# Cross-attention kernel: attention weights of even heads as bytes unpacked on GpSimd, unread TensorE transposes, output biases on TensorE

## The reference, cut to what matters

```python
q = (x @ Wq + bq);  k, v = cond @ Wkv + bkv        # 16 heads of 16 values, 1024 keys
q = _fq_sym(q, axis=-1); k = _fq_sym(k, axis=-1); v = _fq_sym(v, axis=2)
attn = softmax(q @ k.T)                            # per head, 1024 x 1024
attn = _fq_unsigned(attn, axis=-1)                 # attention weights rounded to 0..255, times a scale
out  = (attn @ v) @ Wp + bp
...
return x + (layernorm(x) @ ternary_quantize(Wt).T + bt)
```

## Time and profile before

| | us |
|---|---|
| median of 3 runs (335.58 to 337.09) | 336.85 |
| the profiled execution | 337.5 |
| its span, first to last instruction | 335.7 |
| outside the span | 1.8 |
| first to last exponential of the attention | 129.07 to 301.10, the last ending at 302.30 |
| from there to the end of the span | 33.4 |

### The profile page before, as it was taken

One profiled execution on the slowest core, in us unless ns is written; L12 is line 12 of the kernel. 1 busy time (PEld: TensorE's weight loads), 2 busy tenths in 40 slices (PEclk: granted clock), 3 DMA queues, 4 the chain that ended last, 5 costly groups with the idle time before them and its releaser, 6 DMA issues.

```text
span 335.7 us, 5142 instructions
## 1 busy us (share of the span) xinstructions
PE 268.7 (80%) x1728; PEld 127.3 (38%) x1728; DVE 265.7 (79%) x401; ACT 210.0 (63%) x340; POOL 98.3 (29%) x225
## 2 busy tenths in 40 slices
PE   4993597595156947899999999999999999979670
PEld 4441365473034733233333332333333333338560
DVE  3363799968697878999999899899999999973850
ACT  1100125435533178999999999999999999992210
POOL 2350424476603011221222212222222122211634
PEclk9999559987555977555555555555555555558998
DMA  7824000039100001999999999999999999995011
GB/s 255 276 94 126 0 3 0 0 59 161 34 0 0 0 2 37 196 182 206 185 200 178 215 172 212 184 212 164 227 167 219 197 188 190 199 184 109 16 49 63
DMA packets 148618, 43.34 MB, mean 129 GB/s; under 512 B 143216, under 2 KB 147696, under 8 KB 148592
## 3 DMA queue, kind: packets, MB, share of 16 engines
q1 hardware_dynamic: 146496, 39.60, 65.4%
q0 software_dynamic: 768, 2.10, 1.8%
q10 hardware_dynamic: 1328, 1.32, 1.2%
HBM read 5.25 MB, written 2.10 MB: 22 GB/s over the span
## 4 chain that ended last, share of the span: by engine, by line
issue 36%; DVE 18%; PE 17%; POOL 16%; ACT 6%; DMA 6%; POOLq 1%; ACTq 0%; DVEq 0%
POOL ebias L421 8%; PE ps L1175 5%; PE ps L1158 4%; PE ps L1047 3%; DMA ksplit<-in_x 3%; DVE nmax L878 2%; ACT ctxT L566 2%; POOL scratch L369 2%; PE ps L1150 2%; POOL rstd L375 2%; POOL xs L432 2%; DMA xs<-scratch 2%; POOL out L446 1%; DVE stats L850 1%; ACT kv L557 1%
## 5 line engine op out<-in xcount | busy, mean ns | idle before, releaser
L878 DVE TENSOR_REDUCE nmax<-ps 128x1 f32<-128x1024 f32 x128 | 156.3, 1224 | 16.5 <-PE ps L1175 11.6
L1175 PE MATMUL ps<-keysT,kv 64*128 64x512 bf16 x256 | 130.1, 614 | 9.2 <-ACT ctx L566 1.9
L566 ACT ACTIVATE ctx<-ps,ebias,qscale 128x1024 int16<-128x1024 f32 x64 | 76.9, 1203 | 5.4 <-POOL ebias L421 3.5
L566 ACT ACTIVATE ctxT<-ps,ebias,qscale 128x1024 int16<-128x1024 f32 x64 | 77.0, 1203 | 4.0 <-POOL ebias L421 2.5
L1204 PEld LDWEIGHTS ps<-vals,ksplit 128*128 128x128 f16 x1024 | 36.9, 105 | 100.6 <-issue 100.3
L421 POOL TENSOR_SCALAR ebias<-nmax,qcur 128x1 f32<-128x1 f32 x128 | 33.8, 264 | 136.2 <-DVE nmax L878 127.2
L1204 PE MATMUL ps<-vals,ksplit 128*128 128x16 f16 x1024 | 47.7, 176 | 0.8 <-DVE krest L923 0.8
L475 ACT COPY hT<-ps 128x256 f32<-128x256 f32 x11 | 4.1, 372 | 46.5 <-PE ps L1039 46.5
L1175 PEld LDWEIGHTS ps<-keysT,kv 64*128 64x128 bf16 x256 | 16.3, 107 | 21.8 <-ACT ctx L566 8.1
L543 ACT COPY hT<-ps 128x512 f32<-128x512 f32 x8 | 4.7, 586 | 22.5 <-PE ps L1150 22.5
L1022 PE MATMUL ps<-wkv_s,ctxT 128*128 128x512 f32 x32 | 16.4, 668 | 0.7 <-ACT ctxT L469 0.7
(11 more groups left out here) (176 smaller groups left out, 316.1 us busy)
## 6 DMA issues: line engine op xcount, KB each, us to landing
ctx<-in_ctx SPq DMA_DIRECT2D x2, 512.0 KB, 4.9
ksplit<-in_x ACTq DMA_DIRECT2D x1, 1024.0 KB, 10.9
xs<-scratch SPq DMA_DIRECT2D x1, 1024.0 KB, 5.6
wkv_s<-in_L_xattn_Wkv SPq DMA_DIRECT2D x1, 512.0 KB, 8.1
ksplit<-ctx SPq DMA_TRANSPOSE x32, 4.7
ksplit<-ctxT SPq DMA_TRANSPOSE x32, 4.9
bkv_b<-in_L_xattn_bkv ACTq DMA_DIRECT2D x1, 256.0 KB, 11.4
wt_s<-in_L_ffn_weight SPq DMA_DIRECT2D x1, 256.0 KB, 9.4
```

The costliest lines, as they stand in the source:

```text
L566: a.activation(prob_of(w)[:, (u % 2) * NK:(u % 2 + 1) * NK], score_banks(k, u), ACT.Exp, bias=ebias[:, u % 4:u % 4 + 1], scale=qscale[:, t ...
L878: v.tensor_reduce(nmax[:, u % 4:u % 4 + 1], score_banks(k, u), AX.X, ALU.max, negate=True).then_inc(max_ready, 1)
L1175: last = m.matmul(ps[:, bank + b, :], qT[rows, t, u // 2, :], keysT[rows, u // 2, 512 * b:512 * b + 512], start=True, stop=True)
```

## The change

1. Even heads' weights are written as bytes, odd heads' still as 16-bit integers. A pair then fills 1536 16-bit columns, so its one DMA transpose moves 12 blocks, where it was 16. In the four blocks of the even head each 16-bit value holds two neighbouring bytes.
2. POOL unpacks these four blocks (1024 bytes for each partition) to 16-bit integers in `byteT`, in the loop after every even head's bias, for the pair that began 6 heads earlier (`UNPACK_LAG`). `weigh` waits for the unpacking in even heads and for the DMA in odd ones.
3. `WEIGH_LAG` goes from 6 to 7.
4. Ahead of each `weigh` in the loop PE does 4 bf16 transposes of the identity (`FILLERS`) into the unused half of the product's bank. Nothing reads them. The 7 heads in the tail have none.
5. The output biases `bp` and `bt` come in as a matmul of one contraction row (256 columns, fp32) for each tile, ahead of the projection and the ternary product. DVE's `x4 = xs + bt` and POOL's `xs + bp` go, as does the copy into `qcur`.

```diff
-WEIGH_LAG = 6
+PT = 4
+UNPACK_LAG = 6
+WEIGH_LAG = 7
+FILLERS = 4
...
+            def unpack(t, u):
+
+                pair_turned(pool, t, u // 2)
+                if not (first_tile(t) and u < 2 * PT):
+                    pool.wait_ge(pv_done, count(*before(t, u, 2 * PT)))
+                g.tensor_copy(byteT[:, (u // 2) % PT, :, :, :],
+                              rawT[:, (u // 2) % PAIRS, 0:KT // 2, :].bitcast(U8).rearrange(
+                                  "p b (q j) -> p b j q", j=2)).then_inc(unpacked, 1)
+
             def attention(t, k):
-                if not first_tile(t):
-                    pool.wait_ge(bias_ready, t * H)
-                g.tensor_copy(qcur[:, :], qscale[:, t, :]).then_inc(qcur_ready, 1)
-                pool.wait_ge(qcur_ready, t + 1)
                 for u in range(H):
                     exp_bias(t, u)
-                    if u == H // 2:
-                        g.tensor_tensor(xs[:, t, :], xs[:, t, :], bp_b[:, :], ALU.add).then_inc(x3b_ready, 1)
+                    if u % 2 == 0 and not (first_tile(t) and u < UNPACK_LAG):
+                        unpack(*before(t, u, UNPACK_LAG))
...
+                if u % 2 == 0:
+                    probs = prob_of(w)[:, 0:NK // 2].bitcast(U8).rearrange("p (b q j) -> p b q j", q=P, j=2)
+                    s_in = score_banks(k, u).rearrange("p (b j q) -> p b j q", j=2, q=P)
+                else:
+                    probs, s_in = prob_of(w)[:, NK // 2:PW], score_banks(k, u)
...
-                step(v.tensor_tensor(x4[:, G * g:G * g + G, :], xs[:, G * g:G * g + G, :],
-                                     bt_b[:, :].unsqueeze(1).broadcast_to([P, G, D]), ALU.add))
...
+                    if bias is not None:
+                        m.matmul(out, onesf[0:1, :], bias[0:1, :], start=True, stop=False)
...
-            def weigh(t, k, u):
+            def weigh(t, k, u, fillers=True):
 
-                pair_turned(pe, t, u // 2)
+                if u % 2 == 0:
+                    pe.wait_ge(unpacked, t * NP + u // 2 + 1)
+                else:
+                    pair_turned(pe, t, u // 2)
...
+                if fillers:
+                    idle = ps[:, PV_BANKS[k % NS], D:2 * D].bitcast(BF16)
+                    for i in range(FILLERS):
+                        m.transpose(idle[:, i * P:(i + 1) * P], identb[:, :], identb[:, :])
```

More of the change, by code:

```diff
@@ L177, in build @@
         ebias = sb("ebias", [P, 4])
[L178 to L181, removed]
+        PW = NK + NK // 2
+        prob_low = ctx[:, :, :].rearrange("p r d -> p (r d)").bitcast(I16)[:, 0:2 * PW].rearrange("p (w x) -> p w x", x=PW)
+        prob_high = ctxT[:, :, :].rearrange("p c n -> p (c n)").bitcast(I16)[:, 0:2 * PW].rearrange("p (w x) -> p w x", x=PW)
+        rawT = ksplit[:, :, :, :].rearrange("p a s d -> p (a s d)").bitcast(I16)[:, 0:PAIRS * PW].rearrange(
             "p (w r q) -> p w r q", w=PAIRS, q=P)
+        byteT = sb("byteT", [P, PT, KT // 2, 2, P], I16)
         lsum = sb("lsum", [P, NT, H])
@@ L330, in attention @@
                         sp.wait_ge(pv_done, count(*before(t, 2 * w + 1, 2 * PAIRS)))
-                    sp.dma_start_transpose(probT[:, w % PAIRS, :, :], prob_of(w)).then_inc(turned[w % PAIRS], 16)
+                    sp.dma_start_transpose(rawT[:, w % PAIRS, :, :], prob_of(w)).then_inc(turned[w % PAIRS], 16)
             sp.wait_ge(qT_full, NT)
@@ L447, in scatter_output @@
                                          x4[:, t, :], None).then_inc(stored, 16)
+            for u in range(H - UNPACK_LAG, H, 2):
+                unpack(NT - 1, u)
             fourth_root(0)
@@ L953, in add_ternary @@
                 dve.wait_ge(tern_full, g + 1)
-                v.tensor_tensor(tokens_of(x4, g), ps[:, PRODUCT_BANKS[g], :], tokens_of(x4, g), ALU.add).then_inc(x4_ready, 1)
-            dve.wait_ge(x3b_ready, NT)
+                v.tensor_tensor(tokens_of(x4, g), ps[:, PRODUCT_BANKS[g], :], tokens_of(xs, g), ALU.add).then_inc(x4_ready, 1)
             add_projection(0)
@@ L1151, in turn_group, with product_group @@
                 last.then_inc(full, 1)
-            def product_group(g, lhs, w, bank, need, full):
+            def product_group(g, lhs, w, bank, need, full, bias=None):
                 pe.wait_ge(need, g + 1)
                 for i in range(G):
+                    out = ps[:, bank, i * D:(i + 1) * D]
+                    if bias is not None:
+                        m.matmul(out, onesf[0:1, :], bias[0:1, :], start=True, stop=False)
                     for c in range(C):
-                        last = m.matmul(ps[:, bank, i * D:(i + 1) * D], lhs[:, g % 2, i * C + c, :], w[:, c, :],
-                                        start=(c == 0), stop=(c == C - 1))
+                        last = m.matmul(out, lhs[:, g % 2, i * C + c, :], w[:, c, :],
+                                        start=(c == 0 and bias is None), stop=(c == C - 1))
                 last.then_inc(full, 1)
@@ L1201, in weigh @@
                     pe.wait_ge(att_ready, t - 1)
+                if fillers:
+                    idle = ps[:, PV_BANKS[k % NS], D:2 * D].bitcast(BF16)
+                    for i in range(FILLERS):
+                        m.transpose(idle[:, i * P:(i + 1) * P], identb[:, :], identb[:, :])
                 out = ps[:, PV_BANKS[k % NS], u * HD:(u + 1) * HD]
                 for r in range(KT):
-                    last = m.matmul(out, probT[:, (u // 2) % PAIRS, (u % 2) * KT + r, :].bitcast(F16), vals[:, r, u * HD:(u + 1) * HD],
+                    if u % 2 == 0:
+                        probT = byteT[:, (u // 2) % PT, r // 2, r % 2, :]
+                    else:
+                        probT = rawT[:, (u // 2) % PAIRS, KT // 2 + r, :]
+                    last = m.matmul(out, probT.bitcast(F16), vals[:, r, u * HD:(u + 1) * HD],
                                     start=(r == 0), stop=(r == KT - 1))
@@ L1241, in late_weigh @@
             def late_weigh(u):
-                weigh(NT - 1, NT - 1, u)
+                weigh(NT - 1, NT - 1, u, fillers=False)
             pe.wait_ge(exp_done, NT * H)
```

16 lines of the change are left out of this document (9 added, 7 removed).

## The result

| | before | after |
|---|---|---|
| median, us | 336.87 | 399.57 (397.84 to 400.64, 4 runs) |
| ratio | | 1.187, 95% interval 1.181 to 1.192 |
| span of the profiled execution | 335.7 | 396.8 |
| first to last exponential starts | 172.0 | 213.9 (127.09 to 341.00) |
| a head (before: mean of the 127 steps; after: tiles 2 to 8) | 1.354 | 1.710 |

The account below looks back on a forecast made before the run. The round trip through three score buffers, no engine, was taken as the bound. Attention -11.0, heads before the rise +1.2, tail +5.1, fp32 transposes -0.5 sum to -5.2: 337.5 to 332.3, median about 331.5; range 323 to 350 us.

Parts of the forecast that it names:

- The bound before: Attention: no engine but the round trip through three score buffers, 4.03 us, sets the step, 1.343 us a head.
- the round trip's 1.20: Attention: with scores to maximum at the 2.4 GHz distance the round trip becomes 3.59 us, 1.20 a head.
- I expect the rise within a few heads: Attention: unread transposes make PE dense, so its clock rises soon after the eighth head; rise and hold 0.60.
- the rival: Attention: the clock doesn't rise, PE at 1.2 GHz takes 1.65 us a head, 378 us in all; chance 0.13.
- Denser than then, so I expect it to hold: Attention: with transposes PE at 2.4 GHz is denser than when the clock fell at 131.1, so it stays high.
- 1.26 us a head at full clock: Attention: step down from 1.354 us, ends 1.20 and 1.31; 117 heads gain 0.094 each, -11.0 us.
- Bytes, cast, 12 blocks: Attention: byte exponential 1.20 us, cast 1.00, 12 blocks landing after 4.0; worth nothing alone, keeps the DMA from being next.
- The cast's price: POOL's unpacking: 1.00 us for 1024 elements, from the line between one-operand rows of 256 and 2048; upper end 2.03.
- Tail +5.1 (0 to +7): After the attention: bias matmuls add 2.7 us ahead of ternary and 2.7 after, less 0.3 for waits.
- +0.9: Tail: two bias matmuls of two records each, 0.226 us a record, add 0.9 us to a product group.
- the changing clock: Attention: the clock rises and falls again, heads at a mean of 1.43 us, 351 us in all; chance 0.12.
- -5.1 with a tail of +7: Slow end of the likeliest case: attention gain at 1.31 us a head plus the longest tail, given as 338 us.

Follow-up runs that it names:

- b_split: Kernel before with a head's two score matmuls in different halves of the rows (half the scores not the reference's): 330.55 us, ratio 0.983.
- rows128: Changed kernel with score matmuls over all 128 rows, both heads summed, so not the reference's scores: 358.8 us in one execution.
- fill_mm: Changed kernel with each head's four unread transposes replaced by four unread bf16 matmuls of the same 128 columns and rows: 397.72 us in one execution.
- rows128_no_fill: Changed kernel with score matmuls over all 128 rows (not the reference's scores) and no unread transposes: 375.64 us in one execution.
- zeros_fill: Changed kernel with output biases back on POOL and DVE, scores over 128 rows, the other head's query rows zero (correct scores): 350.0 us, ratio 1.037.
- zeros_plain: Changed kernel without unread transposes, output biases back on POOL and DVE, scores over 128 rows with zeroed query rows: 361.26 us, ratio 1.072.
- hot: Kernel before with 6 unread transposes a head ahead of each weigh, 14 a head in the first six heads: 393.2 us, ratio 1.169.
- zeros_spread: Changed kernel, biases on POOL and DVE, 128-row scores with zeroed query rows filled by plain 64-row copies behind odd heads' biases: 339.0 us, ratio 1.005.
- bias128: Changed kernel without unread transposes and with bias matmuls over 128 rows instead of one: 348.77 us in one execution.
- bias_back: Changed kernel with both output biases added on POOL and DVE as before, no bias matmuls, transposes kept: 378.15 us, ratio 1.119.
- no_fill: Changed kernel with FILLERS = 0, no unread transposes, all else as changed: 363.8 us.
- fill12: Changed kernel with 12 unread transposes a head for 4, all else as changed: 492.16 us.

## Why the prediction was wrong

- *The bound before*: right. b_split takes 0.4 us of score time out at an unchanged clock, and the step falls to 1.23 in its first two tiles, near the round trip's 1.20, until the DMA is next.
- *"I expect the rise within a few heads"*: the step that failed. The clock was 0.50 from 137 to 336 us, with TensorE busy for 198.57 of 199.00, so that a head took 1.71 and not 1.26. I read the rise at 127.7 as the effect of a dense TensorE, and it came while 32 transposes over all 128 rows ran; the attention's longest work is 64-row matmuls. With the same instructions over 128 rows the clock did rise (rows128). The observation stood in the rival's own line, "score matmuls that use 64 rows only", at 0.13. The rival's 378 was this case with an attention of 1.65 a head (measured 1.71) and a tail that was too short.
- The Trainium skill's rule that transpose-mode work doesn't count as busy in the same way ("TensorE: Matmul & The Clock Gate", Part 4) gave the right outcome here. The mechanism is not borne out: fill_mm changes nothing, and transposes hold the clock once scores are 128 rows wide (rows128 against rows128_no_fill, zeros_fill against zeros_plain).
- *"Denser than then, so I expect it to hold"*: wrong for 64-row scores (hot loses it after a tile and a half, though denser still), right for 128-row ones.
- *1.26 us a head at full clock*: too low. rows128 took 1.30, zeros_spread 1.344; the odd head's bias behind the cast is late.
- *Bytes, cast, 12 blocks*: right in price (1.203, 1.036, 3.7) and in that the DMA was not the bound. The cast's price is partly luck: its line went through an fp32 copy and a memset, which reads nothing. Bytes, cast and lag cost 5.7 us in the attention.
- *Tail +5.1 (0 to +7)*: measured +21.2. The term was mis-sized: +1.56 a group for +0.9, and no case had the clock fall in mid-tail. With 128-row biases the tail is +5.3 over before. Without one-row biases the tail's clock is 0.91 or more (bias128, bias_back), with them 0.69 in the changed kernel and 0.73 in no_fill; but fill12 has them at 0.91, with a tail still 12.8 over before. So the rows' price at a high clock is shown, and why the clock falls in one such tail and not in another stays open.
- *Two slips in the working*: half the heads at 1.65 and half at 1.26 are 1.455 in the mean, not 1.43, so that the changing clock comes to 354, outside the range; and -5.1 with a tail of +7 adds up to 339.5, not 338. Neither bears on what failed.
- *The sum*: of the 61.1 us between the spans, 36 are the transposes, 21 the tail, 6 bytes and cast, and -2 the earlier start.

Open: whether any number of transposes between 64-row matmuls lifts the clock; 4 and 12 a head don't. And whether two 64-row matmuls side by side, with transposes between the pairs, would: no run has both.

## What to carry to other kernels

Before counting on TensorE's clock, look at how many of the 128 rows its matmuls use, in the shapes of the profile's groups: a busy TensorE with 64-row scores stayed at 1.2 GHz with 4 or 12 unread transposes a head, and fell back to it with 6. Unread work on TensorE is a bet with an uneven stake: at 1.2 GHz, once TensorE no longer waits, each transpose costs 0.1 us of the step. Where a wait is a matmul's length, two matmuls in different halves of the rows shorten it at either clock (0.61 for 1.03, 0.39 for 0.59), without a bet.

## What was not expected of the hardware

- Same instructions with 4 unread transposes a head, 64 or 128 rows in the scores: clock 0.50 or 1.00 for 150 us; rows of zeros count as rows (zeros_fill).
- Two 512-column matmuls in different row halves take 0.61 us together at 1.2 GHz (b_split), 1.03 in the same half.
- A one-row fp32 matmul of 256 columns costs a tile 0.78 us at 2.4 GHz (1.68 for 0.90), one of 128 rows 0.39 (bias128).
- On POOL 512 bf16 columns took 1.563 us as a product with a scalar per row, 0.605 as a copy of 64 rows.
